# One-hots for counting edges: one edge column and a per-partition scalar in place of 30 columns and two tensors

## The reference, cut to what matters

```python
m  = h[src] * e                                           # layer 0: weighted sum of the sources' rows
ft = segment_sum(m, dst) @ W.T + b
seg_sum, seg_max, cnt = ...segment_*(edge_attr, src)      # layer 1: sum, maximum and mean by source
msg = hw[etype, src] / deg[dst]                           # layer 2: one weight matrix for each relation
a   = softmax over the edges of dst (leaky_relu(el[src] + er[dst]))   # layer 3: attention
```

## Time and the profile before

| | us |
|---|---|
| median of 3 runs | 24838.34 (24823.15 to 24846.76) |
| span of the profiled execution, first to last instruction | 21400.8 |
| median less span: what lies outside the first and the last instruction | 3437.5 |
| GpSimd busy | 16823.9 (79%) |
| VectorE busy | 8437.1 (39%) |
| TensorE matmuls busy | 4183.5 (20%) |

### The profile page before, as it was taken

One profiled execution on the slowest core, in us unless ns is written; L12 is line 12 of the kernel. 1 busy time (PEld: TensorE's weight loads), 2 busy tenths in 40 slices (PEclk: granted clock), 3 DMA queues, 4 the chain that ended last, 5 costly groups with the idle time before them and its releaser, 6 DMA issues. The chain is left out here.

```text
span 21400.8 us, 135402 instructions
## 1 busy us (share of the span) xinstructions
PE 4183.5 (20%) x27708; PEld 3439.5 (16%) x27708; DVE 8437.1 (39%) x31691; ACT 2199.2 (10%) x10623; POOL 16823.9 (79%) x13464
## 2 busy tenths in 40 slices
PE   1111677777760000000061000000000000000000
PEld 1111566656650000000040000000000000000000
DVE  5555666666655455454431111111113222222223
ACT  0000444444440000000010000000000000000000
POOL 7888777777778888888856777777777787787777
PEclk9999755555555555555555555555555555555555
DMA  2111111111102222222221111111112111111112
GB/s 52 36 33 36 33 27 27 27 27 27 27 24 74 67 69 74 66 69 74 66 64 53 45 45 45 45 45 45 46 47 32 46 46 46 46 46 46 42 46 46
DMA packets 660027, 993.34 MB, mean 46 GB/s; under 512 B 393615, under 2 KB 447856, under 8 KB 629104
## 3 DMA queue, kind: packets, MB, share of 16 engines
q0 software_dynamic: 430432, 388.76, 9.6%
q10 hardware_dynamic: 28944, 432.98, 4.9%
q1 hardware_dynamic: 200192, 167.64, 2.9%
HBM read 466.94 MB, written 521.52 MB: 46 GB/s over the span
## 5 line engine op out<-in xcount | busy, mean ns | idle before, releaser
L338 POOL DMA_INDIRECT att_G<-att_table,att_idx x3240 | 3909.3, 1207 | 988.9 <-issue 986.9
L338 POOL DMA_INDIRECT rel_G<-rel_table,rel_idx x3240 | 3726.7, 1150 | 1203.7 <-issue 986.8
L338 POOL DMA_INDIRECT wsum_G<-h_table,wsum_idx x2160 | 3725.8, 1725 | 751.0 <-issue 732.2
L606 POOL DMA_INDIRECT by_src<-sort_row,sort_place_i x3240 | 3139.7, 969 | 987.4 <-issue 987.4
L448 DVE TENSOR_TENSOR_SCAN rel_S<-rel_same,rel_S,rel_G 128x60 f32<-128x60 f32 x3456 | 823.6, 318 | 3901.5 <-DMA rel_G<-rel_table,rel_idx 3901.5
L747 PE MATMUL pG<-sort_counts,sort_lowTf 128*128 128x98 f32 x6484 | 2211.3, 442 | 0.0
L338 POOL DMA_INDIRECT ahead_rows<-h_table,wsum_idx x1020 | 1773.6, 1739 | 310.8 <-issue 310.8
L492 PE MATMUL wsum_C<-wsum_high,wsum_low 128*128 128x98 bf16 x6480 | 568.5, 283 | 5788.6 <-DVE wsum_high L368 5788.6
L747 PEld LDWEIGHTS pG<-sort_counts,sort_lowTf 128*128 128x128 f32 x6484 | 1692.7, 319 | 0.0
L426 DVE TENSOR_TENSOR_SCAN att_er<-att_same,att_er,att_er_in 128x60 f32<-128x60 f32 x54 | 18.5, 342 | 3719.3 <-DMA att_G<-att_table,att_idx 3719.3
L492 PEld LDWEIGHTS wsum_C<-wsum_high,wsum_low 128*128 128x128 bf16 x6480 | 522.1, 143 | 5834.9 <-DVE wsum_high L368 5834.9
(11 more groups left out here) (362 smaller groups left out, 11319.2 us busy)
## 6 DMA issues: line engine op xcount, KB each, us to landing
scan_att<-att_S ACTq DMA_DIRECT2D x54, 1980.0 KB, 7.2
scan_wsum<-wsum_S ACTq DMA_DIRECT2D x54, 1920.0 KB, 6.8
scan_pool<-pool_S ACTq DMA_DIRECT2D x36, 2880.0 KB
scan_rel<-rel_S ACTq DMA_DIRECT2D x54, 1920.0 KB, 6.8
pool_row<-by_src SPq DMA_DIRECT2D x36, 1485.0 KB
sort_feat<-in_attr SPq DMA_DIRECT2D x54, 960.0 KB
by_src<-sort_row,sort_place_i POOLq DMA_INDIRECT x3240
rel_G<-rel_table,rel_idx POOLq DMA_INDIRECT x3240
```

The lines of the kernel that those rows point to most:

```text
L338: pool.indirect_dma_start(out=G[s][:, j, :], out_offset=None, in_=table, in_offset=bass.IndirectOffsetOnAxis(ap=idx[s][:, j:j + 1], axis=0 ...
L606: pool.indirect_dma_start(out=by_src, out_offset=bass.IndirectOffsetOnAxis(ap=place_i[s][:, j:j + 1], axis=0), in_=row[s][:, j, :], in_off ...
```

## The change

The one-hots of a group are made by 60 short instructions in place of 2 long ones. Each short one compares the 128 (or 98) numbers of `iota_b` with one number per partition, taken from a column of `parts`, and writes the row of one column. Since that number is read as a scalar of 4 bytes, `parts` becomes 32-bit; the cast that fills it has the same number of elements. The semaphores stay: `oh_ready` is raised by the last of the 60.

```diff
-                    parts = sb(f"{NAME}_parts", [P, 2, SIDE], BF16, c)
+                    parts = sb(f"{NAME}_parts", [P, 2, SIDE], F32, c)
...
                             dve.wait_ge(oh_used, n + 1)
-                            part = lambda m, w: parts[:, m, g * HL:(g + 1) * HL].unsqueeze(2).to_broadcast([P, HL, w])
-                            iota = lambda w: iota_b[:, 0:w].unsqueeze(1).to_broadcast([P, HL, w])
-                            v.tensor_tensor(low[b][:], iota(P), part(0, P), ALU.is_equal)
-                            v.tensor_tensor(high[b][:], iota(HT), part(1, HT), ALU.is_equal).then_inc(oh_ready, 1)
+                            for j in range(HL):
+                                at = g * HL + j
+                                v.tensor_scalar(low[b][:, j, :], iota_b[:], parts[:, 0, at:at + 1], None, ALU.is_equal)
+                                last = v.tensor_scalar(high[b][:, j, :], iota_b[:, 0:HT], parts[:, 1, at:at + 1], None, ALU.is_equal)
+                            last.then_inc(oh_ready, 1)
```

## The result

The kernel with the change takes 25612.45 us (median of 4 runs, 25608.44 to 25617.53), the kernel before beside it 24830.75 us (24806.91 to 24846.76). The ratio is 1.0315, with an interval of 1.0301 to 1.033: slower by 782 us, where 995 us faster was forecast. The range (23,720 to 24,900) missed it.

What follows compares the result with a forecast made beforehand. GpSimd's queue of gathers was taken to set the pace. Gains of 484 us in stage one and 511 in stage two, together 995, took 24838 to 23843 us; range 23,720 to 24,900.

Steps and rivals of the forecast that it cites:

- the pace of the short operations on VectorE: Stage one's one-hots: 360 short operations started 0.165 us apart take 59.4 us a chunk.
- the 3437.5 us: Time between the profiled span of 21400.8 us and the measured median, taken to lie around the span and stay unchanged.
- stay far below: Stage two: VectorE busy some 77 us a chunk after the change, under GpSimd's 108.5.
- What frees GpSimd: Gathers beside the one-hots no longer held up: 28 us a chunk back in stage one, 14.2 in stage two.
- the sum: Gains of 484 us in stage one and 511 in stage two, together 995 us.
- The hand-over between two back-to-back operations: Short operations hold what GpSimd needs for a few tens of ns and hand it over between two of them.
- the rival of the full shut-out: GpSimd is shut out for the whole row of short operations in both counting stages: 1026 us slower, 25,864; chance 16%.
- the partial one: Hand-over works only sometimes, a transfer passing every 1.5 to 4 us: 24,100 to 25,400 us; chance 7%.
- VectorE waits for GpSimd: Stage one: each transfer delays a short operation by 0.18 us, so 59.4 us a chunk become 69.4.
- The stop at the top of the loop: Longer loop body makes VectorE stand still at each pass: 2.4 us a chunk added in stage one.
- VectorE becomes the bound: Operations don't overlap, 0.25 us each: 128 us a chunk in stage one, stage two's gain kept, 24,455; chance 7%.
- The 158 us: Upper end of the likeliest range: VectorE at 96.4 us a chunk and 2 us friction more in both stages.

Runs made afterwards that it cites:

- setting 25: Sessions of measurement in which the kernel before takes 24.8 ms (24,858, 24,839 and 24,854 us in three of them).
- e13: The change itself, unchanged, against the kernel before in setting 21: 20370.7 us beside 21391.35, ratio 0.9523.
- setting 21: Sessions of measurement in which the same kernel before takes 21.4 ms (21,403 and 21,391 us in two of them).
- e18: The change, with GpSimd waiting after every fourth gather of the counting stages until it has landed, in setting 25: 25898.09 us (one run).
- e3: The kernel before, with `high` made by 30 short operations a group and `low` by the long one, in setting 25: 24569.97 us, ratio 0.9882.
- e11: The kernel before plus 58 one-element writes behind each group of one-hots, in setting 25: 24907.61 us, ratio 1.003.
- e17: The change, with stage two's comparisons using a constant instead of the per-partition number, in setting 25: 25314.84 us (one run).
- after: The profile of the kernel with the change, unchanged, in setting 25; its profiled run took 25617.53 us.
- e8: The kernel before, with the long comparisons reading iota from PSUM, in setting 25: 24416.66 us, ratio 0.9824.
- e12: The change, with the counting stages' indirect gathers replaced by plain transfers of the table's first 128 rows, in setting 25: 22222.84 us, ratio 0.8947.
- e14: The change, with stage two's comparisons using a constant instead of the per-partition number, in setting 21: 20458.33 us.

## Why the prediction was wrong, by its steps

**The step that failed is the pace of the short operations on VectorE (360 x 0.165 us), and the reading of the 3437.5 us that hid it.** The forecast priced them at 59.4 us a chunk, 69.4 with what gathers hold, 73.5 at most. In setting 25 a chunk of stage one takes 141.6 us (its multiplications start at 412.6 and 554.2). Late starts beside the rows of 60 gathers cost VectorE 1,158 us in stage one, 2,184 us of distances less 1,026 in e13, or 64 a chunk; 78 (what VectorE takes in setting 21, see below) + 64 = 142. Stage two takes 4754 / 36 = 132 us a chunk where 108.5 was forecast, and where VectorE was to "stay far below" with some 77.

*"Around it lie 3437.5 us, taken as unchanged."* This was the error that could have been seen. 3.4 ms around a span have no place in a profile whose executions have 1.7 us around theirs. The trace was of setting 21, the three times of setting 25, and they lie inside the program: 3,082 us in the scatter stage (7282 less 4200), 354 behind stage two. With the scatter stage's price in setting 25 in sight, one could have seen that short operations beside indirect transfers are what setting 25 makes dear. The rows 7 that gave 0.165 us are of that very stage, in setting 21.

*What frees GpSimd:* right. In setting 21 the gathers' mean is 1216 ns (forecast near 1.2 us), a chunk of stage one takes 93.2 us (94), one of stage two 106.9 (108.5). The gain in setting 21 is 1,021 us where the sum said 995. The hand-over between two back-to-back operations works, so the rival of the full shut-out falls in both settings, and the partial one with it: L338 has 946 ns in setting 25. That the full shut-out was priced at 25,864, only 252 us from the 25,612 measured, is chance.

*VectorE waits for GpSimd:* mis-sized. The 0.24 us are in the rows (0.50 instead of 0.24), but they overlap the next start and cost nothing: 1,026 / 6,462 x 360 = 57.2 us for 360 operations, not 69.4. *The stop at the top of the loop:* 2.4 us in all of stage one instead of 2.4 a chunk. VectorE therefore takes 1669 / 18 less 260.2 / 18, or 78.3 us, a chunk in setting 21, not 92.3, and was not level with GpSimd.

*VectorE becomes the bound*, the rival at 7%, has the right engine and sign in stage one, but its mechanism (operations that do not overlap, 0.25 us each) is not what happens. It priced 128 us there and left stage two its gain; the runs show 142, and a loss of 380 us in stage two.

*A slip in the range.* The 158 us up to 24,000 are 4.4 us in 36 chunks; by the text's own terms they are 4.4 x 18 + 2 x 36 = 151. Rounded to the next hundred it is 24,000 either way.

*Why before is spared.* Its 64 scans and its long comparisons hold GpSimd up, so the row of gathers is broken while VectorE works, and while the row runs free VectorE waits 57.1 us and has nothing to issue. The protection would be a side effect of the very loss that the change removes. That breaks keep the comparisons on time is shown by e18; that before's holds act as such breaks is only argued, from e3, and e11 speaks against it in part, since its writes are late between holds. A rival is not told apart: before makes the one-hots of a chunk with 12 instructions, and e3 has only 30 short ones in a row, perhaps too few to be caught.

**Open.** What sets the settings apart, and what the 0.70 and 1.40 us are. VectorE, TensorE and, in the scatter stage, ScalarE get their instructions late. What begins the late stretch may be a number of instructions and not a time: it begins 9.8 to 11.3 us into a full row with the change's comparisons, after 58 to 68 of them; 5.7 to 8.8 us into it with those of e17, after 46 to 75; and in e11 after 36 writes that take half a microsecond. That was not tested. The transfers don't: GpSimd's own pitch stays 1.25 to 1.27 us, and each landing follows its gather by 1.0 to 1.3 us throughout a row. That some path to the engines fills up with the work of indirect transfers fits the runs, but none shows which; the transfers that bring code are not it, as their packets show. Whether recording the trace has a part in it was not tried either.

## What to carry to other kernels

Compare the span of the profile with the time that you are to predict before anything else: if they differ by more than a few microseconds, the trace is of another execution than the time, and the difference can sit in stages that the trace shows at another pace. Freeing a resource also removes the pauses that its owner was forced to make; ask what ran well because of them (here that is argued, not shown). And to keep VectorE from holding GpSimd's transfers up, moving one operand (to PSUM: 20,355 us in setting 21, 24,417 in setting 25, faster than before in both, in setting 25 also by 1,220 us faster than the change beside it) was safer than cutting two long instructions into sixty.

## What the runs showed of the hardware

In setting 25, from about 10 us into an unbroken row of 60 indirect transfers until 9 us behind it, VectorE starts a short comparison mostly every 0.70 or 1.40 us (after); before that some 60 start at their usual pace. TensorE starts a weight load or matmul every 1.40 us (e8). Empty writes of one element start 4 to 6 at a time, 0.73 us apart (e11). Plain transfers from the same queue do nothing of the kind (e12), and breaks of 2.2 us after every fourth indirect one prevent it (e18). No packet of code is on record in such a stretch (443 to 526 us of the change), so it is not the fetch of instructions. A comparison with one constant for all partitions starts 0.11 us after the last one, with a number per partition 0.16 us (e14, e13). An operation that a gather stretches from 0.24 to 0.50 us lets the next one start on time.
